# Standard deviation through the u product, router bias in an evacuation, five C pairs moved from VectorE to GpSimd, and the first table moved to chunk 7

## The reference, cut to what matters

```python
x = x + ssm(layernorm(x))      # x is (2, 2048, 256), 16 states for each of the 256 features
x = x + moe(layernorm(x))      # 8 experts, hidden 1024, one expert for each token

# ssm
B_t, C_t = x @ W_B.T, x @ W_C.T
dt = softplus((x @ W_dt1.T) @ W_dt2.T + b_dt2)
A_bar = exp(dt[..., None] * A); B_bar = (A_bar - 1) / (A + 1e-08) * x[..., None] * B_t
h = a_t * h + b_t              # a scan over the 2048 steps
y = sum over states of h * c_t + D_skip * x

# moe
selected = argmax(softmax(x @ Wr + br))
out = gelu(x @ W1[e] + b1[e]) @ W2[e] + b2[e]     # with e = selected, token by token
```

## Time and profile before

| | |
|---|---|
| median of 3 runs | 729.58 us (729.41 to 732.17) |
| profiled execution | 729.98 us, span 728.2 us |
| start of chunk 7 on VectorE (its j = 0) | 396.87 us |
| first expert matmul on TensorE | 448.56 us |
| TensorE / VectorE / ScalarE / GpSimd busy | 94% / 76% / 65% / 64% of the span |
| granted TensorE clock, mean | 0.979 of full speed |

### The profile page before, as it was taken

One profiled execution on the slowest core, in us unless ns is written; L12 is line 12 of the kernel. 1 busy time (PEld: TensorE's weight loads), 2 busy tenths in 40 slices (PEclk: granted clock), 3 DMA queues, 4 the chain that ended last, 5 costly groups with the idle time before them and its releaser, 6 DMA issues.

```text
span 728.2 us, 17484 instructions
## 1 busy us (share of the span) xinstructions
PE 682.6 (94%) x5826; PEld 575.7 (79%) x5827; DVE 554.0 (76%) x998; ACT 472.6 (65%) x987; POOL 462.6 (64%) x584
## 2 busy tenths in 40 slices
PE   8799899899999997999998889999999999999997
PEld 7677677777787685777776679898999999977776
DVE  7889999999989989999998989888343434344441
ACT  3986998998998997898995587433333323233451
POOL 3798988988978967898886487223343434343331
PEclk9699999999999999899998999999999999999999
DMA  7967642352243243243231168711111111111010
GB/s 235 282 233 261 204 148 73 103 165 93 94 147 117 90 142 91 59 148 117 80 126 59 59 190 286 293 37 52 58 52 58 48 58 45 58 38 33 25 45 15
DMA packets 42290, 82.21 MB, mean 113 GB/s; under 512 B 4825, under 2 KB 12638, under 8 KB 42209
## 3 DMA queue, kind: packets, MB, share of 16 engines
q1 hardware_dynamic: 37600, 68.58, 28.5%
q0 software_dynamic: 4608, 12.59, 5.6%
HBM read 69.35 MB, written 13.37 MB: 114 GB/s over the span
## 4 chain that ended last, share of the span: by engine, by line
PE 64%; POOL 11%; issue 11%; ACT 9%; DVE 3%; DMA 1%; POOLq 0%; SPq 0%; DVEq 0%; ACTq 0%
PE WW L1167 16%; PE misc L1204 15%; PE WW L1050 11%; PE YY L1088 8%; POOL w_sb L662 8%; ACT w_sb L830 4%; ACT Csb L820 3%; PE misc L1199 2%; PE WW L1161 2%; POOL b_sb L643 2%; PE misc L964 2%; PE misc L976 1%; DVE w_sb L1331 1%; PE YY L1136 1%; DMA w_sb<-c_rows 1%
## 5 line engine op out<-in xcount | busy, mean ns | idle before, releaser
L662 POOL TENSOR_TENSOR w_sb<-w_sb,Csb 128x512 f32<-128x512 f32 x206 | 260.2, 1274 | 69.4 <-DVE w_sb L1331 61.5
L1050 PE MATMUL WW<-b_sb,xin 64*128 64x130 f32 (+2 forms) x2304 | 202.7, 293 | 27.3 <-DVE w_sb L1331 12.8
L1050 PEld LDWEIGHTS WW<-b_sb,xin 64*128 64x128 f32 x2304 | 168.4, 192 | 74.5 <-issue 34.1
L1331 DVE TENSOR_TENSOR_SCAN w_sb<-WW,hlast,w_sb 128x512 f32<-128x512 f32 x156 | 192.4, 1268 | 3.9 <-issue 2.2
L830 ACT ACTIVATE w_sb<-dt,negA 128x512 f32<-128x512 f32 x256 | 170.3, 710 | 12.5 <-DVE w_sb L1331 8.7
L911 ACT ACTIVATE dt<-WW,b1c 128x128 f32<-128x128 f32 x256 | 72.8, 387 | 128.7 <-PE WW L1167 122.2
L1088 PE MATMUL YY<-sm,w_sb 128*128 128x128 f32 x1024 | 142.8, 285 | 5.0 <-DVE row L1388 5.0
L724 POOL DMA_INDIRECT y_out<-CbX,ocol x36 | 42.8, 1189 | 141.3 <-DVE CbX L1765 136.6
L1088 PEld LDWEIGHTS YY<-sm,w_sb 128*128 128x128 f32 x1024 | 113.8, 144 | 19.7 <-POOL w_sb L662 3.9
L1204 PE MATMUL misc<-w_sb,dt 128*128 x512 | 115.7, 379 | 0.5 <-issue 0.5
L820 ACT ACTIVATE Csb<-w_sb,invA 128x512 f32<-128x512 f32 x134 | 91.5, 713 | 25.7 <-POOL w_sb L662 23.9
(11 more groups left out here) (305 smaller groups left out, 826.4 us busy)
## 6 DMA issues: line engine op xcount, KB each, us to landing
w_sb<-c_rows SPq DMA_DIRECT2D x86, 256.0 KB, 3.4
CbX<-c_rows SPq DMA_DIRECT2D x42, 256.0 KB, 3.4
w_sb<-w_in SPq DMA_DIRECT2D x20, 512.0 KB, 6.0
token_rows<-row SPq DMA_DIRECT2D x8, 1024.0 KB, 5.2
w_sb<-w_in SPq DMA_DIRECT2D x24, 256.0 KB, 5.1
xin<-x_in SPq DMA_DIRECT2D x8, 512.0 KB, 4.0
w_sb<-x_in SPq DMA_DIRECT2D x7, 512.0 KB, 8.0
b_sb<-b_in SPq DMA_DIRECT2D x1, 780.0 KB, 9.1
```

Source lines behind the costliest of these rows:

```text
L662: eng.tensor_tensor(hc[g % NHC], hb_of(g), Csb[i % NCS][:, :], ALU.mult).then_inc(s_hcp, 1)
L1050: return eng.matmul(to[:, a:a + width], x_rows[rows, k, h * P:(h + 1) * P], band[rows, k, at:at + width], start=start, stop=not start, ski ...
L1331: eng.tensor_tensor_scan(hb_of(g) if pooled(g) else w_of(g), w_of(g), A[g % NA], hlast[(q - 1) % 2][:, h * N + n:h * N + n + 1] if q % NC ...
```

## The change

- `u_product` takes an 18th row: GpSimd copies the standard deviations (4 numbers a partition) into `cbrow`, and the table has ones in that row. `u_times_x` becomes one multiplication of 512 elements where it was two instructions of 256 (add and multiply).
- The router's bias is added by ScalarE in its evacuation of `routeT` (`Identity` with a bias in place of `Copy`); `logits` loses its addition, and its maximum goes to an SBUF tile.
- `VECTOR_UNITS`: chunk 4 loses pair 8; chunks 5 and 6 have pair 8 alone in place of 5 and 12; chunk 7 has 4, 10, 15 in place of 1, 4, 8, 10, 15.
- `first_table`'s five parts move from j = 30 and 31 of chunk 6 to j = 1, 2 and 3 of chunk 7; `keep_ids` moves from j = 15 to 17; the gathers from n = 8, 10, 13 to 9, 11, 13.

```diff
-VECTOR_UNITS = [(1, 6, 9, 12)] + [(5, 8, 12)] * 4 + [(5, 12)] * 2 + [(1, 4, 8, 10, 15)]
+VECTOR_UNITS = [(1, 6, 9, 12)] + [(5, 8, 12)] * 3 + [(5, 12)] + [(8,)] * 2 + [(4, 10, 15)]
...
+                if q:
+                    eng.wait_ge(s_rsx, q)
+                else:
+                    eng.wait_ge(s_sg, 1)
+                eng.tensor_copy(cbrow[:, :, N + 1], sgx[:, (q - 1) * TI:q * TI] if q else sg0[:, :])
                 eng.tensor_tensor(cbrow[:, :, 0:N], brow[b][:, :, 0:N], brow[b][:, :, N:2 * N], ALU.mult)\
...
-                    if last and n in (8, 10, 13):
-                        t = (8, 10, 13).index(n)
+                    if last and n in (9, 11, 13):
+                        t = (9, 11, 13).index(n)
...
-                    eng.activation(routed, source[:, 0:P], ACT.Copy).then_inc(s_free, 1)
+                    eng.activation(routed, source[:, 0:P], ACT.Identity, bias=col("br_row")).then_inc(s_free, 1)
...
-                return eng.matmul(at, cbt[CS * k:CS * k + N + 1, :], table_of_u[CS * k:CS * k + N + 1, :],
+                return eng.matmul(at, cbt[CS * k:CS * k + N + 2, :], table_of_u[CS * k:CS * k + N + 2, :],
...
-                for i in range(2):
-                    k = which + 2 * i
-                    ins = eng.scalar_tensor_tensor(tail[:, k * D:(k + 1) * D], spot(name, q)[:, i * D:(i + 1) * D],
-                                                   std_of(q, k), xin[q % B][:, k, :], ALU.add, ALU.mult)
-                ins.then_inc(s_freev, 1)
+                eng.tensor_tensor(tail[:, :].rearrange("p (i d) -> p i d", d=D)[:, which::2, :],
+                                  spot(name, q)[:, :].rearrange("p (i d) -> p i d", d=D), xin[q % B][:, which::2, :],
+                                  ALU.mult).then_inc(s_freev, 1)
...
-                done(eng.tensor_tensor(mine, rows[:, 0:P].rearrange("p (i e) -> p i e", e=CS)[:, :, 0:E],
-                                       col("br").unsqueeze(1).to_broadcast([P, TI, E]), ALU.add), "rt")
-                done(eng.tensor_reduce(top, mine, AX.X, ALU.max), "rt")
-                eng.tensor_tensor(mine, mine, top.unsqueeze(2).to_broadcast([P, TI, E]), ALU.subtract)\
+                scores = rows[:, 0:P].rearrange("p (i e) -> p i e", e=CS)[:, :, 0:E]
+                done(eng.tensor_reduce(top, scores, AX.X, ALU.max), "rt")
+                eng.tensor_tensor(mine, scores, top.unsqueeze(2).to_broadcast([P, TI, E]), ALU.subtract)\
...
-                    if q == NQ - 2 and j > 29:
-                        first_table(2 * j + gap - 60)
-                        if (j, gap) == (31, 1):
-                            first_table(4)
-                    if last and (j, gap) == (15, 0):
+                    if last and 0 <= 2 * j + gap - 2 <= 4:
+                        first_table(2 * j + gap - 2)
+                    if last and (j, gap) == (17, 0):
                         keep_ids()
```

More of the change, by code:

```diff
@@ L59 @@
 SMALL = dict(ident=P, logA=KD * N, wr=KD * CS, umask=1, wcd=KD * CBD, wdt2=D, skip=D, band=HALF + 1, last=1,
-             b1=E * KH, tri=P, e_less8=E, e_base=E, tok0=NT, j128=32, tile_no=ENTRIES - SURE, turned=2 * len(SPLIT), br=E)
+             b1=E * KH, tri=P, br_row=1, e_less8=E, e_base=E, tok0=NT, j128=32, tile_no=ENTRIES - SURE, turned=2 * len(SPLIT))
 OFF = {}
@@ L1361, in mean_of @@
                 return mvx[:, (q - 1) * TI + i, 0:1] if q else mv[0][:, i, 0:1]
-            def std_of(q, i):
-                return sgx[:, (q - 1) * TI + i:(q - 1) * TI + i + 1] if q else sg0[:, i:i + 1]
             def u_times_x(q, which):
@@ L1371, in u_times_x @@
                     wait(eng, s_z, 2 * q)
-                    if q:
-                        eng.wait_ge(s_rsx, q)
-                    else:
-                        eng.wait_ge(s_sg, 1)
-                for i in range(2):
-                    k = which + 2 * i
-                    ins = eng.scalar_tensor_tensor(tail[:, k * D:(k + 1) * D], spot(name, q)[:, i * D:(i + 1) * D],
-                                                   std_of(q, k), xin[q % B][:, k, :], ALU.add, ALU.mult)
-                ins.then_inc(s_freev, 1)
+                eng.tensor_tensor(tail[:, :].rearrange("p (i d) -> p i d", d=D)[:, which::2, :],
+                                  spot(name, q)[:, :].rearrange("p (i d) -> p i d", d=D), xin[q % B][:, which::2, :],
+                                  ALU.mult).then_inc(s_freev, 1)
             def finish_rows(q, which):
@@ L1399, in logits @@
                 rows, mine = spot("route", q), lg[:, q * TI:(q + 1) * TI, :]
-                top = rows[:, 256:256 + TI]
+                top = nm[0][:, :]
                 eng.wait_ge(s_full, HOP["route", q] + 1)
-                done(eng.tensor_tensor(mine, rows[:, 0:P].rearrange("p (i e) -> p i e", e=CS)[:, :, 0:E],
-                                       col("br").unsqueeze(1).to_broadcast([P, TI, E]), ALU.add), "rt")
-                done(eng.tensor_reduce(top, mine, AX.X, ALU.max), "rt")
-                eng.tensor_tensor(mine, mine, top.unsqueeze(2).to_broadcast([P, TI, E]), ALU.subtract)\
+                scores = rows[:, 0:P].rearrange("p (i e) -> p i e", e=CS)[:, :, 0:E]
+                done(eng.tensor_reduce(top, scores, AX.X, ALU.max), "rt")
+                eng.tensor_tensor(mine, scores, top.unsqueeze(2).to_broadcast([P, TI, E]), ALU.subtract)\
                    .then_inc(s_lg, 1)
@@ L1825 @@
     skip[N::CS] = a["attn_D_skip"]
+    skip[N + 1::CS] = 1.0
     wr = np.zeros((D, CS), f)
@@ L1837 @@
         tri=(one[:, None] < one[None, :]).astype(f),
+        br_row=np.pad(a["ffn_br"], (0, CS - E))[one % CS].astype(f)[:, None],
         e_less8=np.tile(np.arange(E, dtype=f) - E, (P, 1)),
@@ L1844 @@
                         .astype(f), (P, 1)),
-        turned=np.tile((np.arange(2 * len(SPLIT)) % 2 * (FAR_A + 1)).astype(f), (P, 1)),
-        br=np.tile(a["ffn_br"], (P, 1)))
+        turned=np.tile((np.arange(2 * len(SPLIT)) % 2 * (FAR_A + 1)).astype(f), (P, 1)),)
     assert list(parts) == list(SMALL)
```

## The result

In rounds on one chip with the kernel before, the changed kernel took 728.97 us (median of 20, 723.46 to 733.97) against 730.32 us (20 runs, 729.36 to 733.53). The ratio is 0.9956, with a 95% interval of 0.9937 to 0.9974: 1.4 us faster between the medians, 3.2 us by the ratio. 723.6 us was forecast, with a range to 728.0, so the measured median lies outside it.

The account below looks back on a forecast made before the run. TensorE was taken to bound a chunk's middle, VectorE with ScalarE and GpSimd its ends. Gains of 2.6, 1.8 and 4.2 us (8.6), less 2.6 in chunk 7, gave -6.0 from 729.58: 723.6 us, range 717.5 to 728.

Parts of the forecast that it names:

- +2.6 us, bounds -2.6 and +4.1: Chunk 7 gets longer: 1.8 us for pair 10's late C row, 2.3 for the gather, less 1.5 absorbed.
- the lower clock level in chunk 7: Rival: table's gap slows TensorE's clock at n = 1 to 7, 738.6 us; chance 0.08, shared with the late C row.
- The prediction's own sign of being wrong: Wrong if chunk 7's first scan isn't 6 us earlier, TensorE's clock is low after 400 us, or gathers delay TensorE at n = 13.
- The price of 2.2 us a pair: Chunk 7 at the lower clock: a make_w group costs 1.1 us more, with add_y and hop about 2.2 a pair.
- the forecast's 6.0 us are used up at three pairs: Clock rival in chunk 7: three pairs at the lower clock cancel the whole gain; seven make it 9 us slower.
- Standard deviation and bias: End of each chunk: 0.36 us from u_times_x, 0.56 with the router bias; 2.6 us by the end of chunk 4.
- C pairs: Chunk 4's moved pair worth 0; chunks 5 and 6 gain 1.8 us up to n = 8 of chunk 6, bounds 0 and 2.7.
- The table leaving chunk 6: End of chunk 6: chunk 7 starts 4.2 us earlier, 3.6 if the clock stays low, 5.1 if high.
- The C row: Chunk 7: pair 10 waits 3 to 4 us for its row behind early1 and weight loads, coming 1.8 us later.
- The gather at n = 11: Chunk 7: second gather delays GpSimd's products behind pair 10 by 2.3 us, 1.5 of them absorbed.
- GpSimd as the bound of chunks 5 and 6: Rival: GpSimd, with 15 pairs in a row, bounds chunks 5 to 7; 726.6 us, chance 0.20 together with no change.
- The expert phase: After the first expert matmul: keeps its length of 279.6 us and moves with its start.

Follow-up runs that it names:

- the best version: Changed kernel with the first table back in chunk 6 and SP's wait and weight loads behind n = 12's C row: 722.42 us, on another chip 724.02.
- two gaps filled: Changed kernel with cbt's transpose done 13 times and nine more at n = 2, in TensorE's waits in chunk 7's head: 724.33 us; C row moved too, 724.66.
- one gap filled: Changed kernel with chunk 7's transpose of cbt done 13 times in place of once, in front of TensorE's 1.65 us wait: 728.91 us, ratio 0.9967.

## Why the prediction was wrong

**The step that failed** is the one for chunk 7, "+2.6 us, bounds -2.6 and +4.1", and with it the chance of 0.08 for the rival "the lower clock level in chunk 7". From its start to the first expert matmul chunk 7 was 8.7 and 9.1 us longer than before in the two profiles (60.4 and 60.7 us against 51.7), outside both bounds. What the runs show in place of the forecast's wait and gather is that rival, at its place and by its mechanism: the table's gap, a `make_w` group of 2.74 us, the return after some pairs. By the times and mean clocks 15 of 32 executions went this way; two of them are profiled. The prediction's own sign of being wrong, a low clock after 400 us, is there too. My argument against it was that "the same gap stood at the end of chunk 6 and the clock recovered behind it within one or two pairs". One profile can't carry this, and it was misread: the fall that the prediction took, from 387.7 to 395 us, begins before the table's first instruction at 391.59; behind the table's gap the clock fell once more, from 401 to 405 us. In chunk 7 the fall lasted 17 and 20 us, some three pairs and more. The price of 2.2 us a pair was right (5.73 - 3.46 = 2.3), and so was the point from which it decides, "the forecast's 6.0 us are used up at three pairs". Between the middles of the two groups lie 730.1 - 724.2 = 5.9 us. I had let the rival run through seven pairs to 738.6, and the range ended at 728.

**The sum came out in the group near 724**, 724.2 us against 723.6, and that is in part luck. The standard deviation with the bias and the pairs of chunks 4 to 6 bring 3.6 and 3.5 us by themselves, 7.1 together and more than the 6.0 of the whole forecast; the rest of the change then brings nothing. In the profile of 723.69 us with the C row moved chunk 7 is 2.0 us longer than before (388.58 to 442.30), near the 2.6, but without the wait for the C row and with 7 us at the lower clock, so by other terms. The terms one by one:
- *Standard deviation and bias*, 0.56 us a chunk: chunk 3 went from 50.66 us to 50.16, 0.50 less. `u_times_x` is 16 instructions of 0.68 us, forecast 0.67. By itself this half is worth 3.6 us (730.1 - 726.46), where 0.4 + 5 to 7 x 0.56 give 3.2 to 4.3.

```profile
L1374 DVE TENSOR_TENSOR tail<-misc,xin 128x512 f32<-128x512 f32 x16 | 10.9, 678 | 5.5 <-PE misc L937 5.5
```

- *C pairs*, 1.8 us by chunk 6: mis-sized. 3.5 us measured, of which 1.2 is a fall of the clock at the end of chunk 6 that the profile before has and this one hasn't. The pair of chunk 4 was worth 0, as forecast, and chunk 5's 1.1 us less lies within the range given.
- *The table leaving chunk 6*, 4.2 us: its 3.3 us are real at that place, and the clock's share comes without it. Chunk 7 begins 7.9 and 9.3 us earlier (389.01 and 387.57 against 396.87), forecast 8.6. But the 3.3 us are spent again, as forecast, in chunk 7, so that the move as a whole is worth half a microsecond at most, which the counts can't tell from nothing.
- *The C row*: forecast, a wait of 3 to 4 us before pair 10, and a row that comes last. It was 2.21 + 0.38 = 2.6 us, in the profile's row of it (424.42 to 432.91, 8.49 us, against 7.39 in the earlier trace rows), and the row ended the wait. Nearly the wait that was forecast, and cheap, about half a microsecond, in the group near 724.

```profile
424.42 8.49 DMA w_sb<-c_rows
```

- *The gather at n = 11*, "2.3 us, 1.5 of them absorbed": not found. At n = 10 the best version isn't faster; the older place has a price that I hadn't counted, ScalarE's 2.78 us behind the gather.
- *GpSimd as the bound of chunks 5 and 6*: it wasn't. It has 4.1 and 3.6 us idle in those stretches, less than the 7.3 and 13.6 of the earlier trace rows, and VectorE kept its gain. (The prediction's "some 5 to 8 us idle in each stretch" misreads: it is 7.3 to 13.6.)
- *The expert phase*: 729.0 - 449.40 = 279.6 us, as forecast.

The product on GpSimd takes 1277 ns after, in chunk 5's stretch, and 1274 before:

```profile
L667 POOL TENSOR_TENSOR w_sb<-w_sb,Csb 128x512 f32<-128x512 f32 x30 | 38.1, 1277 | 3.9 <-DVE w_sb L1336 3.8
```

It didn't get slower with more products beside VectorE's scans. The rule that was weighed in the prediction (the Trainium skill, SBUF — State Buffer, "Who interferes with whom": a VectorE instruction contends with GpSimd's reads of SBUF when both of its inputs are in SBUF, and doesn't with one at most) is not contradicted, as the scan takes one input from PSUM.

The lower clock is told of by the Trainium skill too (TensorE: Matmul & The Clock Gate, "HAM oscillation — how this bites in real kernels"): a kernel whose bursts of matmuls are parted by waits begins each burst cold. The profile after agrees as to the direction, with two waits of 1.65 and 1.12 us ahead of the fall. The first profile with the table back doesn't: two waits of 1.19 and 2.12 us, and no fall.

**What is shown and what is open.** Shown: in the kernel as changed, the table at the head of chunk 7 is what brings the times near 730 (put back: none of 10, besides the odd one; kept: 15 of 32), and in the profiles those are the ones in which TensorE stays at its lower clock for 14 us or more. Supported but not closed: that TensorE's idle time there is the link (two gaps filled: 1 of 12 above 727 us, against 20 of 44 in the same kernels without; one gap filled, which left the idle time nearly as it was: no effect); and that the late C row adds some 2.6 us to the upper group, with a second fall in three of four profiles. Open: why the clock comes back after 7 us in one execution and after 17 in the next, why as long an idle time at the end of chunk 6 mostly does no harm, and why chunk 7's two pairs put back bring times of 726 to 730 with the table at its old place.

## What to carry to other kernels

Before work is moved off the bound engine into a quieter place, look at what it leaves idle next: three microseconds of VectorE's work, moved, cost this kernel six in every other execution, through the clock, at a place where TensorE is full behind it. When two groups of times appear, count them by the granted clock of each run, take the profile of one as that group's and not the kernel's, and profile an execution of the other before saying what sets them apart. A delay that is harmless by itself (the C row) isn't so behind one that has used up the slack.
